# Selective scan in a 1024-token block: the order of one chunk's work on four engines

## The reference

```python
xz = silu(in_proj_w @ x + b);  x_ssm, res, gate = split(xz, 3)
xf = silu(conv3(x_ssm));  dbc = dbc_w @ xf          # dt, B_t, C_t for each head
x_h, dt, B_t, C_t = (gathered by perm)
h = exp(dt * A) * h + (dt * B_t) * x_t              # for each of 1024 tokens
y = sum over states (h * C_t) + D * x
y = y[inverse perm] * silu(gate) + res;  x = x + silu(out_proj_w @ y + b)
x = x + sum over experts (weight * (norm(x) @ expert_w + expert_b))
```

## Time and profile before

| | |
|---|---|
| median of 3 runs (lowest, highest) | 1070.61 us (1068.48, 1070.85) |
| profiled execution, its own time | 1064.97 us |
| its span | 1063.2 us |
| busy share of the span: PE, DVE, ACT, POOL | 88%, 73%, 48%, 48% |
| projections, scan, last part (from the timeline) | to about 250, to about 510, to 1063 us |

### The profile page before, as it was taken

One profiled execution on the slowest core, in us unless ns is written; L12 is line 12 of the kernel. 1 busy time (PEld: TensorE's weight loads), 2 busy tenths in 40 slices (PEclk: granted clock), 3 DMA queues, 4 the chain that ended last, 5 costly groups with the idle time before them and its releaser, 6 DMA issues.

```text
span 1063.2 us, 15454 instructions
## 1 busy us (share of the span) xinstructions
PE 930.4 (88%) x4658; PEld 718.6 (68%) x4658; DVE 771.3 (73%) x2001; ACT 508.6 (48%) x924; POOL 505.9 (48%) x563
## 2 busy tenths in 40 slices
PE   4999999986687678666499999999999999999997
PEld 3887888874454445444367777777777777877776
DVE  5768887534677778775458787787787877878775
ACT  2777877664666665666223333332333323333330
POOL 2066666775887877788650333313333132330000
PEclk8999999996777887778689999999999999999999
DMA  5335674476254343334331131401314013140001
GB/s 162 119 89 171 190 191 147 116 175 177 76 144 126 98 120 109 117 108 156 126 133 44 33 145 39 147 30 39 138 39 158 21 38 138 39 158 20 20 1 39
DMA packets 63687, 110.05 MB, mean 104 GB/s; under 512 B 18538, under 2 KB 44436, under 8 KB 60564
## 3 DMA queue, kind: packets, MB, share of 16 engines
q1 hardware_dynamic: 56468, 91.41, 27.4%
q0 software_dynamic: 7168, 18.03, 5.9%
HBM read 61.51 MB, written 47.92 MB: 103 GB/s over the span
## 4 chain that ended last, share of the span: by engine, by line
PE 69%; DVE 7%; ACT 7%; issue 5%; POOL 5%; DMA 4%; ACTq 0%; SPq 0%; DVEq 0%; another core or an unknown queue 0%; POOLq 0%
PE bank L1322 31%; PE bank L1064 8%; PE bank L1230 4%; PE bank L1255 4%; PE bank L1185 3%; ACT xf L937 3%; PE bank L1283 2%; PE bank L1074 2%; PE bank L1194 2%; POOL sm L708 2%; PE bank L1197 2%; PE bank L1122 2%; PE bank L1092 2%; DMA score_scratch<-score 1%; PE bank L1267 1%
## 5 line engine op out<-in xcount | busy, mean ns | idle before, releaser
L763 POOL TENSOR_TENSOR ssm<-ssm,rg 128x512 f32<-128x512 f32 x30 | 35.2, 1192 | 269.7 <-DVE ssm L1799 269.7
L751 POOL DMA_INDIRECT xtm<-y_scratch,idxu x120 | 119.2, 993 | 68.6 <-issue 34.2
L1322 PE MATMUL bank<-wexph,xhl 128*128 128x512 f32 x512 | 144.9, 405 | 0.1
L1322 PE MATMUL bank<-wexph,cr 128*128 128x512 f32 x512 | 143.4, 401 | 0.1
L708 POOL TENSOR_TENSOR sm<-sm,rg 128x512 f32<-128x512 f32 x96 | 122.4, 1275 | 30.0 <-DVE rg L1701 20.1
L1701 DVE TENSOR_TENSOR rg<-rg,bank 128x512 f32<-128x512 f32 x128 | 83.2, 681 | 60.6 <-ACT rg L921 39.9
L1322 PEld LDWEIGHTS bank<-wexph,xhl 128*128 128x128 f32 x512 | 93.8, 189 | 23.4 <-DVE xf L1903 2.0
L1322 PEld LDWEIGHTS bank<-wexph,cr 128*128 128x128 f32 x512 | 93.4, 189 | 22.0 <-DVE ysb L1903 1.7
L921 ACT ACTIVATE rg<-dists,aown 128x512 f32<-128x512 f32 x128 | 84.7, 714 | 0.0
L1322 PE MATMUL bank<-wexpl,xhl 128*128 128x512 f32 x256 | 80.6, 396 | 0.0
L1322 PE MATMUL bank<-wexpl,cr 128*128 128x512 f32 x256 | 80.3, 395 | 0.0
(11 more groups left out here) (303 smaller groups left out, 2111.9 us busy)
## 6 DMA issues: line engine op xcount, KB each, us to landing
xin<-in_x SPq DMA_DIRECT2D x16, 1024.0 KB, 5.3
res_gate_scratch<-rg SPq DMA_DIRECT2D x16, 1024.0 KB, 10.9
rg<-res_gate_scratch SPq DMA_DIRECT2D x8, 2048.0 KB
y_scratch<-ysb SPq DMA_DIRECT2D x16, 512.0 KB, 3.6
out<-stage SPq DMA_DIRECT2D x16, 512.0 KB, 2.7
rows_scratch<-xr SPq DMA_DIRECT2D x8, 580.0 KB
rows_scratch<-stage SPq DMA_DIRECT2D x8, 580.0 KB
bc_scratch<-r SPq DMA_DIRECT2D x16, 288.0 KB
```

The source lines that it names most:

```text
L751: pool.indirect_dma_start(out=xtm[:, t, h * P:(h + 1) * P], out_offset=None, in_=y_d[b // GB].rearrange("q p s c -> (q p s) c"), in_offset ...
L763: pool.tensor_tensor(z[:, k, :], z[:, k, :], rg[:, k, cols], ALU.add).then_inc(z_ready.sem, 1)
L1322: last = pe.matmul(bank[4 + i][:, :], x_[:, k, i * P:(i + 1) * P], w[:, 2 * ep * KC + k:2 * ep * KC + k + KC + 1:KC, :], start=(n + k == 0 ...
```

## The change

On **DVE** a chunk's `whole_kernel(q-1)` moves from behind `times_decay(0)` to behind `rows_low`, `distances` and `times_decay(1)`, and `exponents(q+2)` moves ahead of `times_decay(6)`. On **ACT** all decays of a chunk come first, then `states_by_tile`, then the two `y_rows`. On **PE** `rows_of(q+1)` moves behind the first two products. The running sum `ksum` has two tiles in turn, so POOL's first add waits for `whole_kernel` of chunk q-2 and no longer for that of q-1. In the last batch of projections the first chunk's work is put among them: `sums_of(0)` behind output block 2 of 6, `rows_of(0)` and `times_of(0)` behind block 3, and on DVE the zeroing of the operand tile ahead of the first convolution, `flatten(0)` and `exponents(0)` ahead of the second. The places are made and scattered for each head apart and in fours, in batches 3, 4, 5 and 6, the last four ahead of `softplus_back`. `store_rows(6)` moves from SP to ACT, behind the last projection's `silu_of`, and `softplus_front(6)` on POOL moves behind the first gathers.

```diff
-        ksum = sm[:, 0:4, :].rearrange("p s n -> p (s n)")
+        ksum = [sm[:, 4 * i:4 * i + 4, :].rearrange("p s n -> p (s n)") for i in range(2)]
...
                 if b == NB - 1:
-                    store_rows(b - 1)
                     sync.wait_ge(cr_zero, 1)
...
@@ POOL batch(b) @@
                 deviations(b + 1)
+                if b == NB - 2:
+                    scatter_order(1, 1)
                 if b:
                     softplus_back(b - 1)
...
-                if b == NB - 3:
-                    scatter_order(0)
-                if b == NB - 2:
-                    scatter_order(1)
+                if NB - 5 <= b < NB - 2:
+                    scatter_order(*divmod(b - NB + 5, 2))
...
-            softplus_front(NB - 2)
             pool.wait_ge(order_loaded, 16 * HEADS)
...
             up_to_token(Chunk(0))
+            softplus_front(NB - 2)
             softplus_back(NB - 2)
@@ add_state @@
-                    pool.wait_ge(k_ready.sem, k_ready.at(c.q, 0))
+                    if c.q:
+                        pool.wait_ge(k_ready.sem, k_ready.at(c.q - 1, 0))
@@ ACT batch(NB - 1) @@
                 silu_xf(b, 1)
+                if not ahead:
+                    act.wait_ge(consts_ready, 1)
+                    rows_high(Chunk(0))
+                    block_decays(Chunk(0))
...
+                silu_of(b, 5)
                 if not ahead:
-                    act.wait_ge(consts_ready, 1)
-                    rows_high(Chunk(0))
-                    block_decays(Chunk(0))
-                silu_of(b, 5)
+                    store_rows(b - 1)
@@ ACT body(q) @@
-                decays(c, 2, 4)
                 if q:
-                    y_rows(Chunk(q - 1), 0)
+                    decays(c, 2, S)
+                    states_by_tile(c)
+                    for h in range(HEADS):
+                        y_rows(Chunk(q - 1), h)
@@ PE batch(NB - 1) @@
+                    in_proj(b, par, 1, 3)
                     sums_of(Chunk(0))
-                    dbc_by_tokens(b)
+                    in_proj(b, par, 3, 4)
                     rows_of(Chunk(0))
                     times_of(Chunk(0))
+                    in_proj(b, par, 4, 5)
+                    dbc_by_tokens(b)
                     in_proj(b, par, 5, MI)
@@ PE body(q) @@
+                products(c, 0, 2)
                 if q + 1 < CHUNKS:
                     rows_of(Chunk(q + 1))
-                products(c, 0, 3)
+                products(c, 2, 3)
@@ DVE batch(b) @@
+                if not ahead:
+                    zero_rows(0, NB - 1)
                 convolve(b, 0)
                 if ahead:
                     statistics(own1, b + 1)
+                else:
+                    flatten(Chunk(0))
+                    exponents(Chunk(0))
                 convolve(b, 1)
@@ DVE body(q) @@
                 times_decay(c, 0)
-                if q:
-                    whole_kernel(Chunk(q - 1))
                 if q + 1 < CHUNKS:
                     rows_low(Chunk(q + 1))
                     distances(Chunk(q + 1))
-                for s in range(1, 4):
-                    times_decay(c, s)
+                times_decay(c, 1)
+                if q:
+                    whole_kernel(Chunk(q - 1))
+                times_decay(c, 2)
+                times_decay(c, 3)
...
                     flatten(Chunk(q + 2))
+                    exponents(Chunk(q + 2))
                 times_decay(c, 6)
-                if q + 2 < CHUNKS:
-                    exponents(Chunk(q + 2))
```

More of the change, by code:

```diff
@@ L637, in low_experts, with scatter_order @@
                                    ALU.subtract).then_inc(wexp_low, 1)
-            def scatter_order(h):
-                pool.wait_ge(place_ready, 1)
+            def scatter_order(h, part):
+                pool.wait_ge(place_ready, h + 1)
                 part_waits(pool)
-                for t in range(NT):
+                for t in range(part * TPH, (part + 1) * TPH):
                     pool.indirect_dma_start(
@@ L702, in add_state @@
                     pool.wait_ge(dskip_ready, 2)
-                    pool.wait_ge(k_ready.sem, k_ready.at(c.q, 0))
+                    if c.q:
+                        pool.wait_ge(k_ready.sem, k_ready.at(c.q - 1, 0))
                 else:
                     pool.wait_ge(summed.sem, summed.at(c.q, s))
-                tiles = (v.rearrange("p (t n) -> p t n", n=SUB) for v in (ksum, ee[:, s, :]))
+                tiles = (v.rearrange("p (t n) -> p t n", n=SUB) for v in (ksum[c.two], ee[:, s, :]))
                 total, new = tiles
@@ L1578, in ranks, with places, rows_by_rank @@
                     own.settle()
-            def places():
-                own.did(dve.tensor_reduce(idxb[:, :, :], racc[:, :, :, :], AX.X, ALU.add))
+            def places(h):
+                own.did(dve.tensor_reduce(idxb[:, h, :], racc[:, h, :, :], AX.X, ALU.add))
                 own.settle()
-                for h in range(HEADS):
-                    own.did(dve.tensor_scalar(placef[:, h, :], idxb[:, h, :], float(h * N), None, ALU.add))
+                own.did(dve.tensor_scalar(placef[:, h, :], idxb[:, h, :], float(h * N), None, ALU.add))
                 own.settle()
-                own.did(dve.tensor_copy(place[:, :, :], placef[:, :, :]))
-                own.did(dve.tensor_copy(names, bc(token[:, :, :].rearrange("p t h -> p (t h)"), 2, 16)))
+                own.did(dve.tensor_copy(place[:, h, :], placef[:, h, :]))
+                if h == 0:
+                    own.did(dve.tensor_copy(names, bc(token[:, :, :].rearrange("p t h -> p (t h)"), 2, 16)))
                 own.settle()
                 dve.sem_inc(place_ready, 1)
+            def rows_by_rank():
                 own.did(dve.tensor_copy(idxu[:, :, :], idxb[:, :, :]))
@@ L1600, in places, with zero_rows @@
                 ts(idxb[:, 1, :], idxb[:, 1, :], float(SUB * ST), None, ALU.add)
+            def zero_rows(i, b):
+                for hf in range(2):
+                    dve.wait_ge(mm_full[hf].sem, mm_full[hf].at(b, 0))
+                dve.memset(cr[i].bitcast(F32), 0.0).then_inc(cr_zero, 1)
             RANKS = {1: (0, 4), 2: (4, 8), 3: (8, 12), 4: (12, 16)}
@@ L1712, in whole_kernel @@
                     rr = slice(SUB * i, SUB * i + SUB)
-                    dve.tensor_tensor(kbd[rr, :, rr], ksum[rr, :].rearrange("p (s n) -> p s n", s=ST),
+                    dve.tensor_tensor(kbd[rr, :, rr], ksum[c.two][rr, :].rearrange("p (s n) -> p s n", s=ST),
                                       ee[rr, S - 1, :].rearrange("p (s n) -> p s n", s=ST),
@@ L1749, in _ @@
                 batch(b)
-            for k in range(2):
-                dve.wait_ge(mm_full[k].sem, mm_full[k].at(NB - 1, 0))
-            dve.memset(cr[0].bitcast(F32), 0.0).then_inc(cr_zero, 1)
             first, second = Chunk(0), Chunk(1)
-            flatten(first)
-            exponents(first)
             rows_low(first)
```

29 lines of the change are left out of this document (16 added, 13 removed).

## The result

The changed kernel takes 1092.32 us in the median of 4 runs (1090.19 to 1093.54), the kernel before 1069.69 (1068.48 to 1070.85, 4 runs). The ratio is 1.0232, 95% interval 1.0211 to 1.0253: slower, and by 22.6 us where I had forecast 7.5. The time lies outside my range.

The account below looks back on a forecast made before the run. No engine is full in the scan; a loop of waits through several engines sets 15.22 us a chunk. Terms 6.2 + 1.0 - 0.7 + 1.0 = 7.5 us, on the median of 1070.61, give 1078 us, range 1073 to 1084.

Parts of the forecast that it names:

- Removed: Scan: ACT and other waits leave the loop; if nothing replaced them, POOL's 13.41 us, 1.8 us less a chunk.
- Added, the place: Scan: `whole_kernel(q-1)` behind `distances` makes a new PE and DVE loop; 15.7 us a chunk against 15.22, +6.2 us.
- I take 2.75: Scan, DVE: the two `kbd` instructions together take 2.75 us beside POOL's adds, against 1.38 at the median.
- PE's own work for a chunk is ... 11.1 us: Scan, PE: busy time per chunk at mean clock 0.78; 10.8 us after one product hidden in the gap.
- the loop of PE and DVE: Scan: PE's 10.8 us plus `distances`, times 1, hand-overs and both `kbd`; 15.0 us.
- the loop through POOL: Scan: adds 4 to 6, `dtri`, `times_of`, `distances`, `kbd`, `weigh` and times; 15.05 us, 15.45 with eight hand-overs.
- `exponents(q+2)` no longer waits for times 6: Scan, DVE: listed among the removed waits, with no size of its own.
- My 15.45: Scan: predicted length of the loop through POOL, 15.05 us plus eight hand-overs at 0.05.
- Two loops taken with 0.25 for their meeting: Scan: loops of 15.0 and 15.45 us share `times_of` to `kbd`; some 0.25 added, giving 15.7 a chunk.
- First period +1.0: Chunk before the 13: 13.41 us before, 14.4 taken with the new loop; +1.0 us.
- tail -0.7: End of the scan: most of the last add's 0.89 us wait for DVE goes with decays first; -0.7 us.
- The start +1.0: Ahead of the scan: PE stands 6.6 us, image 6's store lands at 263; second add at 266.9, +1.0 us.

Follow-up runs that it names:

- e15: Kernel before with only ScalarE's (ACT's) order changed, all decays of a chunk first; ratio 0.9798, 13.99 us a chunk.
- e16: e15 with `whole_kernel` put behind `rows_low`, still ahead of `distances`, one sum tile; ratio 0.9790, 13.56 us a chunk.
- e14: Kernel before with e7's scan but one sum tile, everything ahead of the scan as before; ratio 0.9830, 13.79 us a chunk.
- e5: Changed kernel with one sum tile, so POOL's first add waits for `kbd` of the chunk before; ratio 1.0065, 15.24 us a chunk.
- e3: Changed kernel with `whole_kernel(q-1)` back behind times 0, ahead of `rows_low` and `distances`; ratio 0.9887, 14.22 us a chunk.
- e7: Changed kernel with `whole_kernel` behind `rows_low` but ahead of `distances` and times 1; ratio 0.9813, 13.76 us a chunk.
- e12: Kernel before with only `whole_kernel(q-1)` moved behind `rows_low`, `distances` and times 1, one sum tile; ratio 1.0581, 19.64 us a chunk.
- e6: Changed kernel with product 3 done 12 times more a chunk, in PE's pause ahead of `y_of(0)`; ratio 1.0175, 16.64 us a chunk.
- e4: Changed kernel with `exponents(q+2)` back behind times 6, `whole_kernel` still behind `distances`; ratio 1.0245, 17.00 us a chunk.
- e13: e12 with product 3 done eight times more a chunk, in PE's pause ahead of `y_of(0)`; ratio 1.0304, 17.56 us a chunk.
- e1: Changed kernel with the whole scan as before, so only what lies ahead of the scan is changed; ratio 1.0032, 15.38 us a chunk.

## Why the prediction was wrong in size and right in direction

**Removed: right, and under-used.** That ACT's `hx` copies set the pace and that up to 1.8 us a chunk lay there holds: e15 gains 1.23 with ACT's order alone, e16 1.66. Of the other removals, the free first add (second sum tile) is worth nothing (e14) or, with `kbd` in its late place, costs 1.75 (e5); the moved exponents and `rows_of` gain nothing (e14 and e16).

**Added, the place: right, and named rightly.** `whole_kernel` behind `distances` is the cause: e3 and e7 undo it and gain 2.8 and 3.2 us a chunk; e12 does it alone and loses 4.4.

**"I take 2.75" for the pair: mis-sized.** It was 3.25 in the chunk above, 0.5 more. The rows show how: the first `kbd` comes 0.26 us behind the start of an add and ends 0.56 behind its end; the add behind it runs to 407.27, and the second `kbd` ends 0.55 behind that. That is the rule that I had taken from the Trainium skill (SBUF — State Buffer, "Who interferes with whom": whichever comes second is blocked for the whole instruction) with the phases put in; I had taken it to the letter only for the worst phases, 3.9. What I had left at its length of before was lengthened too: `bct`, 0.28 us before. Of the 16 copies in the changed kernel the 13 that started during an add of POOL took 0.97 to 1.13 us, the other three 0.28.

**"PE's own work for a chunk is ... 11.1 us", "10.8": right as a sum, wrong as a model.** I took it from a busy time at a mean clock of 0.78 and let it stand when a pause was put ahead of `y_of(0)`. In the changed kernel the clock was at 0.50 behind that pause in every chunk, and `y_of(0)` took 3.76 us against 1.99 at full clock (e6). For the loop of PE and DVE, e4's chain shows the size: from the end of `times_of` to `y_of(0)` it has 4.0 us, about the 4.2 of the sum, but the rest is 13.0 where I had 10.8. Both `y_of` take 6.16 of it, against 3.74 at full clock in e13. This is the largest of the missing terms: +2.2 us on a loop that I had at 15.0. In the loop through POOL this is the stretch from the end of `kbd` (407.82) to times 4 (412.21), 4.4 us, where I had 3.15 for times 2, 3 and `weigh`: +1.2.

**"`exponents(q+2)` no longer waits for times 6": costed as a gain, and its other side left out.** Ahead of times 6 they put times 6 behind `y_of(1)` and `sums_of`, and add 6 and `dtri` behind that: adds 4 to 6 with the wait take 4.88 us (412.98 to 417.86) where I had 4.1: +0.8. My 15.45 with +0.5, +1.2 and +0.8, less 0.6 for `times_of` (1.36 and not 1.94), is 17.35, against the 17.00 of the chain; the difference is about the 0.4 that I had added for hand-overs, which these stretches hold already.

**Two loops taken with 0.25 for their meeting.** They were three, of 17.0 (changed), 17.05 (e4) and 16.6 us (e6), each through `kbd` behind `distances`. That would be why the clock gave 0.35 and the exponents 0, and why only the place (e3, e7) or one sum tile (e5) opened them all; it is read from the chains of single chunks.

**First period +1.0, tail -0.7.** The first period was 13.2 us as before (288.89 to 302.05, against 13.41): +0. The tail was +0.9.

**The start +1.0: right in kind, the store mis-sized.** PE stood at `sums_of(0)` and the adds came later by the late store: it landed at 266.0 and not 263, and the first add came at 269.2 and not 265.5. PE's wait was 10.65 us and not 6.6, but only because PE came there at 226.45 and not at 231.9; the rows were there at 236.86, earlier than the 238.5 expected, and the store went out at 254.2, as expected behind a `silu_of` at 254.5. So rival (d), whose condition of a longer wait was met, was not the cause: the store took 11.83 us where I had 8.5. That is in part the luck of one execution: in the seven others with this start it took 8.4 to 10.9. Chunk 2 came 4.0 us later; in the measured times the start is 3.4 us (e1).

The scan gives 23.0 of the 27.9 us in the profiled executions where I had 6.2 and 1.0.

## What to carry to other kernels

When a move puts a wait in front of TensorE, count the wait, and then ask what the engine's work behind it would cost at the lower clock; a mean busy time of the old order hides this. It is a risk and not a fixed price: behind the pauses of 3.3 to 4.4 us the clock was low in all 13 chunks, behind e5's of 2.3 to 2.5 in every other one, and there it cost nothing, because another loop was longer. Before a second buffer is given to an engine, ask what it will then run beside: here the earlier adds only lengthened VectorE's instructions. And try the parts of a change alone: one of its moves had all of the gain and another more than all of the loss.

## What was unexpected

Work that nobody needs made the kernel faster: eight products more a chunk, in a pause of 2.3 us, took 2.08 us off (e12 to e13), by PE's clock. And VectorE's copy `bct<-xr`, with only one input, took 0.97 us with POOL adding and 0.28 without. And e5 has nearly the same pause ahead of `y_of(0)` in each chunk, and the clock behind it was low in one and full in the next.
